# Graph kernel, edge phases: a completion signal for every tile of the placing product

## What is computed

```python
score = a_s[:, src] + a_d[:, dst] + aw_e[:, None] * elem[None, :] + ab[:, None]
w = jnp.exp(-jax.nn.relu(score / 20.0))
dst_f = feats[:, dst]
pooled = jax.vmap(lambda wi, fi: seg(wi[:, None] * fi))(w, dst_f)
row_sum = jax.vmap(lambda wi: seg(wi))(w)
out = pooled / row_sum[:, :, None]
...
msg = (h[src] + rel_e) @ weight_neighbor * alpha
agg = jax.ops.segment_sum(msg, dst, num_segments=n)
```

## Time and profile before

| what | us |
|---|---|
| median of 3 runs | 2502.88 (2497.65 to 2503.34) |
| profiled execution, its own time | 2481.36 |
| its span, first to last instruction | 2479.6 |
| window of edge phase 0 | 250 to 946 |
| window of edge phase 1 | 1550 to 2270 |

### The profile page before, as it was taken

One profiled execution on the slowest core, in us unless ns is written; L12 is line 12 of the kernel. 1 busy time (PEld: TensorE's weight loads), 2 busy tenths in 40 slices (PEclk: granted clock), 3 DMA queues, 4 the chain that ended last, 5 costly groups with the idle time before them and its releaser, 6 DMA issues. The chain is left out here.

```text
span 2479.6 us, 40282 instructions
## 1 busy us (share of the span) xinstructions
PE 1639.9 (66%) x9301; PEld 1175.0 (47%) x9301; DVE 1690.6 (68%) x4231; ACT 1080.0 (44%) x2994; POOL 1264.8 (51%) x1217
## 2 busy tenths in 40 slices
PE   0678466565666665289999956466676666766378
PEld 0576244343444444289999954233333333333266
DVE  8997766666666667677778646567777777777811
ACT  0474334443333343212222226676676676664321
POOL 0387566666666660126666610655666565652042
PEclk9889667667666666599999977566677667777689
DMA  3014444444444443289999962555665565663331
GB/s 101 2 5 68 152 107 108 109 108 110 109 108 110 107 98 67 65 281 279 301 303 303 305 213 77 172 164 160 167 165 165 161 167 162 167 169 49 91 87 22
DMA packets 212676, 351.09 MB, mean 142 GB/s; under 512 B 45840, under 2 KB 123980, under 8 KB 212588
## 3 DMA queue, kind: packets, MB, share of 16 engines
q0 software_dynamic: 75616, 167.60, 27.1%
q1 hardware_dynamic: 136972, 182.41, 23.9%
HBM read 318.55 MB, written 31.34 MB: 141 GB/s over the span
## 5 line engine op out<-in xcount | busy, mean ns | idle before, releaser
L1164 POOL DMA_INDIRECT e_rows<-table,e_gidx x880 | 846.5, 962 | 525.2 <-issue 233.1
L1227 DVE TENSOR_TENSOR acc<-acc,e_psO 128x260 f32 (+1 forms) x880 | 463.5, 527 | 274.9 <-DMA edge_rows<-row_out 156.6
L1437 PE MATMUL e_psO<-e_rows,e_oh 128*128 128x260 f32 x880 | 374.5, 594 | 233.4 <-DVE acc L1227 206.0
L1437 PEld LDWEIGHTS e_psO<-e_rows,e_oh 128*128 128x128 f32 x880 | 236.3, 290 | 314.6 <-DVE acc L1227 209.3
L2277 PE MATMUL e_psO<-e_rows,e_oh 128*128 128x456 bf16 x440 | 225.1, 512 | 95.3 <-DVE acc L1227 84.1
L1318 PE MATMUL e_psA<-e_own_of_unit,e_ohT 128*128 (+2 forms) x880 | 104.1, 184 | 188.2 <-issue 80.4
L1318 PEld LDWEIGHTS e_psA<-e_own_of_unit,e_ohT 128*128 128x128 bf16 x880 | 82.0, 103 | 274.6 <-issue 263.3
L1406 ACT ACTIVATE e_rows<-e_psA 128x16 f32<-128x16 f32 x110 | 20.3, 184 | 399.5 <-DVE e_psA L1397 300.8
L788 POOL DMA_INDIRECT records<-ordered,s_chunk x68 | 119.1, 1752 | 110.7 <-DVE s_chunk L615 80.9
L2179 ACT ACTIVATE away<-iota_b,etype 128x200 bf16<-128x200 bf16 x440 | 165.3, 446 | 0.0
L2237 DVE TENSOR_SCALAR e_oh<-iota_b,seg,inverse 128x128 bf16<-128x128 bf16 x440 | 117.9, 337 | 69.3 <-issue 57.7
(11 more groups left out here) (444 smaller groups left out, 3669.6 us busy)
## 6 DMA issues: line engine op xcount, KB each, us to landing
hot_run<-in_L_ffn_w_dram SPq DMA_DIRECT2D x107, 512.0 KB
XN<-in_L_ffn_w_dram SPq DMA_DIRECT2D x85, 512.0 KB
e_edge_row<-edge_rows SPq DMA_DIRECT2D x110, 256.0 KB
e_edge_row<-edge_rows SPq DMA_DIRECT2D x110, 128.0 KB
e_rows<-table,e_gidx POOLq DMA_INDIRECT x880
table<-frow SPq DMA_DIRECT2D x25, 192.5 KB
table<-chunk_steps SPq DMA_DIRECT2D x25, 130.0 KB, 2.2
normed_rows<-Z SPq DMA_DIRECT2D x5, 642.5 KB
```

Of the source, the lines that this page charges most:

```text
L1164: pool.indirect_dma_start(out=rows[:, r, t, 0:width], out_offset=None, in_=table, in_offset=bass.IndirectOffsetOnAxis(ap=gidx[:, r, t:t + ...
L1227: v.tensor_tensor(d, d, psO[:, units * (r % (4 // units)) + j, 0:accw], ALU.add).then_inc(S["added"], 1)
L1437: return pe.matmul(out[:, 0:A0], oh[:, r, t, :], rows[:, r, t, :], start=start, stop=stop)
```

## The change

TensorE signals `summed` behind each of the four tiles, so it counts tiles and no longer groups. POOL waits before each of its four gathers for the same tile of the group four back, VectorE's addition of tile j for tile j. The other waits on `summed` (L1208, L1424, L2183) keep their meaning and count in tiles.

```diff
@@ POOL
-                    back(pool, S["summed"], g, DEPTH)
                     pool.wait_ge(S["gidx_ready"], g + 1)
-                    hold(pool, "pool")
                     for t in range(TPG):
+                        back(pool, S["summed"], g, DEPTH, per=TPG, extra=t + 1 - TPG)
+                        hold(pool, "pool")
                         pool.indirect_dma_start(
@@ VectorE, one-hots of phase 1
-                        back(dve, S["summed"], g, DEPTH)
+                        back(dve, S["summed"], g, DEPTH, per=TPG)
@@ VectorE, additions
-                    if j == 0:
-                        dve.wait_ge(S["summed"], g + 1)
+                    dve.wait_ge(S["summed"], g * TPG + (j + 1) * tpu)
 
                     if not (isinstance(g, int) and g == 0 and j == 0):
+                        hold(dve, "dve")
                         dve.wait_ge(S["added"], g * units + j)
@@ TensorE
                             ins = post["product"](pe, psO[:, units * (r % (4 // units)) + u, :], oh, rows, r, t,
                                                   t % tpu == 0, t % tpu == tpu - 1)
-                        ins.then_inc(S["summed"], 1)
+                            ins.then_inc(S["summed"], 1)
@@ ScalarE, one-hots of phase 0
-                    act.wait_ge(S["summed"], g - (DEPTH - 1))
+                    act.wait_ge(S["summed"], (g - (DEPTH - 1)) * TPG)
@@ ScalarE, relation counts of phase 1
-                back(act, S["summed"], g, DEPTH)
+                back(act, S["summed"], g, DEPTH, per=TPG)
```

## The result

The changed kernel takes 2527.86 us (median of 4 runs, 2523.87 to 2532.05), the kernel before 2502.74 beside it: a ratio of 1.0105, 95% interval 1.0083 to 1.0127, 25 us **longer**. The forecast was 2480; 2528 lies in the range, on the other side. The profiled execution is the changed kernel's 2526.18, while the one shown of before stands 21.5 us under its median.

The account below looks back on a forecast made before the run. The edge phases were taken as bound by engines waiting for each other, every second product's signal coming about 3.4 us late. Gains of 14 us (phase 0) and 9 us (phase 1) made 2502.9 - 23 = 2480 us, range 2430 to 2590.

Parts of the forecast that it names:

- The base reading: Edge phases: POOL sets the pace, and its pauses come from every second product's signal arriving about 3.4 us late.
- The fourth case (a latency): Rival, edge phases: signals simply take 3.4 us in every second group; pauses shrink to the gap, 2277 utmost, 2390 likelier; chance 0.11.
- (3): DVE's additions: no waiting instruction more, one register instruction for a group, hidden behind an addition of 0.42 us.
- (5): POOL's gathers: tile signals give runs of nine in phase 0, 14 us less, and longer short runs in phase 1, 9 less.
- the 23 us: Edge phases: the forecast gain from longer gather runs, 14 us in phase 0 plus 9 us in phase 1; chance 0.37.
- (2): POOL's gathers: three more waits and counts for a group cost nothing while the engine is busy with the gather before.
- Early hold: Rival, POOL's runs: an early tile signal is caught and holds those behind, giving runs of five; 2571 us, chance 0.29.
- Nothing moves: Rival, POOL's runs: all four tiles of every second group are held, runs stay at eight; 2503 within 7 us, chance 0.18.
- Signals cost: Rival, TensorE's signals: three more signals delay the group's fourth; 12 us taken, 2515 us, chance 0.05.

Follow-up runs that it names:

- e2: The changed kernel with POOL waiting once for a group again, DVE still adding tile by tile; 1.0089 of the kernel before.
- e3: The kernel before with TensorE signalling each tile, all engines still waiting for the group's fourth signal; 1.0035 of the kernel before.
- e1: The changed kernel with DVE's additions waiting for the group's last signal again, POOL still waiting tile by tile; 1.0006 of the kernel before.
- d1: The changed kernel with one more semaphore increment of DVE ahead of each addition; 1.0385 of the kernel before with pauses, 1.0057 and 1.0050 without.
- c1: The changed kernel itself run again, in a session without pauses; 1.0014 of the kernel before.
- f1: The changed kernel with DVE's four additions behind the payload instead of between its scores; 1.0127 of the kernel before, with pauses.
- f2: The changed kernel with DVE waiting for two tiles at a time; 0.9997 of the kernel before, with pauses.
- p2: The kernel before with POOL waiting before each gather until the gather two before has landed; 2883.9 us, 1.1654 of the kernel before.

## Why the prediction was wrong

- **The base reading held, as far as it went.** The pauses are bound to late signals: where signals are on time there are none, and the kernel before takes 11% less. The fourth case (a latency) put the time without pauses at 2277 at the utmost; the session alone brought 2222, the change none of it.
- **"Once POOL has issued some gathers without a pause, a signal does not get through" is false as a rule.** 424 gathers went through in a row with signals on time. It describes what was seen in one kind of session; something not in the program belongs to it.
- **The step that failed is (3), what DVE pays.** I wrote "no waiting instruction more, one register instruction for a group, hidden", and that score, exponential and payload wait for the whole group today anyway. The records show 396 small instructions more in phase 0, 3.6 for a group. 322 of them are semaphore instructions: the change puts a `hold` before every addition, which its diff shows and the listing of instructions above leaves out, and I did not count it. Nor are they always hidden: 232 of 2081 took 0.15 to 0.74 us, nearly all from the fourth gather of a run on. I took their price from places outside the runs. In place of nothing, DVE's part costs 11 us over the signals alone (e2 against e3) and 16 us over POOL's part (e2 against e1); one more instruction before each addition costs 2.8% (d1), and with the lateness gone the whole change costs 0.14% (c1). That DVE's longer step delays the next product, and with it POOL's release, is read from the timelines and from the longer pauses; theory 1, which says so, missed the size in e2's pauses, f1, f2 and d1.
- **The gain in (5) did not come.** In phase 0 runs stay at eight and pauses grow by 0.6 us; in phase 1, where runs of four should have grown, there are 28 of them in place of 18 and half as many of eight. Nor did e1 gain, which has the tile signals for POOL without DVE's waits and no loss: its runs in phase 0 are of eight to ten with single gathers between, and the sum is that of the kernel before. So the 23 us did not come even without DVE's waits. The sum has a slip too, which changes nothing here: a ninth gather in phase 1 would give (12.58 + 1.25) / 9 = 1.537 us each, not 1.554, and a bound of 25 us, not 17.
- **(2), POOL's waits at nothing**, was right (e1).
- **Early hold** had "slower", but its reason explains no loss: in phase 0 runs of five did not come. In phase 1 runs of five to seven came in part (25, before 4), but e1 has even more of them (34) and no loss. **Nothing moves** describes e1, not the change. **Signals cost** was sized well: 12 us forecast, 7 to 9 measured in e3, about 3 for the whole change in c1. In e1 it is gone, so it is not what most of the 25 us are made of. The Trainium skill's rule ("TensorE: Matmul & The Clock Gate", section "The cost: per-tile semaphore tail"), 26.3 ns each, would be 17 us; e3 agrees with its sign and shows half of its size.
- The mark that I had set myself was a DVE step in phase 1 beyond 5.4 us. As a median it is not met: two steps there start 5.85 us apart, as before (5.84, pauses included). It is met in the steps that a run catches: one in ten takes over 8.85 us (8.11 before), and from the first to the last addition of a group pass 3.62 us on average in place of 2.96 (3.31 in e2, 2.96 in e3).

The Trainium skill's "Perfetto Trace Analysis", section "Sequencer-only Instruction (DRAIN, etc)", says that the recorded window of such an instruction begins when its semaphores are satisfied. By it the 0.7 us are no waiting for a signal; the ALU_OP at 798.600, which has none to wait for, agrees.

## What to carry to other kernels

Before an engine's one wait is cut into several, look at what its small instructions take at that place and not elsewhere: max beside median in the rows of its queue, and idle time put down to "issue". Where signals come late in bursts, count how often an engine stops for them: two tiles to a wait cost nothing here and four waits 1%. And a stall that makes a tenth of a kernel should be looked for in a second session before changes are built on it.

## What was not expected of the hardware

- The kernel before takes 2222 to 2223 us or 2475 to 2503, and one chip showed both within minutes. For the changed kernel, whose two traces can be compared, all of it lies in the edge phases. With pauses, 46 of 110 product signals of phase 0 are on time in the kernel before and 129 of 440 in the changed one, and small instructions of DVE often take 0.7 us; without, 438 of 440 are on time in the changed kernel, and no small instruction of phase 0 takes over 0.15. What the two kinds of session differ in no run shows; two gathers under way at most (p2) take the lateness away in phase 0 even there. The limit of three was tried only without pauses.
- Whether late signals and slow small instructions have one cause stays open: they come in the same stretches and go together, and no run parts them. So does why phase 0 pauses longer in the changed kernel (3.08 us) than in e2 (2.59), while e1 and e2 together lose about what the changed kernel does; they were profiled in different sessions. And it stays open why two tiles to a wait cost nothing, with 59 pauses of 2.12 us.
- DVE's register and semaphore instructions, 0.02 to 0.06 us, took 0.69 to 0.73 in the stretch shown, behind later gathers of a run, several in a row.
- A gather that has waited for a landing starts 0.78 us after it.

No version tried beats the kernel before; f2_by_halves and e1_pool_by_tile equal it.
